# Early-fusion transformer layer on one core: the softmax sums' products beside the value products, three sum buffers, later scaling, and the FFN weights' transposes in the prologue

## The chip, the core and the metric

One core of a Trainium2 chip runs the whole kernel. Its engines run programs of their own and meet at semaphores: PE (TensorE, matrix products into PSUM), ACT (ScalarE), DVE (VectorE), POOL (GpSimd) and SP (SyncE, which here issues every DMA). The metric is the device time of one execution in microseconds (us); less is better.

## What is computed

Sixteen items, each of 1024 image positions (29 features) and 77 text tokens, give 1101 rows of 128 numbers. One attention layer with 8 heads of 64 and one gated FFN with a shared path and 8 experts follow. Cut to what matters:

```python
h = concat([einsum('bsf,fd->bsd', x, W) + pe, text_rows], axis=1)     # 16 x 1101 x 128
y = layernorm(h)
q, k, v = (einsum('bsd,hdk->bhsk', y, w) for w in (wq, wk, wv))
probs = softmax(einsum('bhsk,bhtk->bhst', q, k) / 8)
h = h + concat_heads(einsum('bhst,bhtk->bhsk', probs, v)) @ head_kernel
flat = layernorm(h) * ln_scale + ln_bias
out_shared = swiglu(flat @ shared_in_w.T) @ shared_out_w.T + shared_out_b
routed = cnt @ expert_out_bias                  # the two best experts of the better group
for e in range(8):
    routed = routed + comb[:, e] * (swiglu(flat @ expert_in_w.T) @ expert_out_weight[e].T)
return h + out_shared + routed
```

The text rows come from three tables; one index is a running count modulo 8.

## The kernel before

**Items, steps and tables.** The attention of an item goes by pairs of heads (4), chunks of up to 368 queries (3) and tiles of 128 keys (9): 108 steps. In each step PE makes the scores of one tile for both heads of the pair (`score`, L853 and L855) and ACT their exponentials, `probs` (L960). Behind the scores of its step PE does the work that a table of letters puts there: `k` projections of queries and keys for the next pair (L749), `m` products whose row maxima DVE takes (L758, L1022), `v` values (L742), `p` output projection of the item before (L785), `t`, `g`, `c`, `u` its layer norm, gate and FFN, `x`, `e`, `f` embedding and layer norm of the next item, `r` the row of maxima (L762), `s` the sum's products (L776), and `|` a run of value products (L872). There is a table for the prologue (BEFORE), the first item (FIRST), items 1 to 14 (EVERY), the last (LAST) and the epilogue (BEYOND). `plan` turns a table into a list of units per step, and every engine walks the same list, each in its own order.

**Value products.** A run `|` weighs the values of five tiles (first run of a chunk) or of four (second). Each product writes 64 of the 128 columns of TensorE, so the two heads of a pair run side by side. All other products but the sums' use the whole width.

**Sums.** The softmax denominators of a chunk are added up by POOL, tile by tile, into `sums` (L1246 for the first two tiles, L1250 for the others). At step 3 of the next chunk the unit `s` sums over the partitions with four products of 32 columns each (L776, `ones` as weights). ACT copies the result (L916), SP sends it through a narrow tile (`inv_cols`), DVE inverts it two steps on (`INVERT`), SP stores it and spreads it back over the partitions (`sums<-inverse_rows`). POOL then scales the heads' output (`scale`, L1221). `sums` has two buffers; `scale` of chunk q stands at step 0 of chunk q + 2. The last two chunks of an item are scaled at steps 0 and 8 (`SCALE_LAST`) of the next item, whose projections (`p`) wait for it.

**PSUM.** Two banks hold scores, one the values' output, five (`LANES`) go round among all other units: a unit on PE waits until the unit that had its bank five units before has been read out.

**Startup.** A block of its own loads weights, works out the text rows, transposes the FFN weights on PE (26 transposes, L463) and splits them and the attention weights into a high and a low part (ACT L471 to L484, DVE L556 to L570). All engines meet at its end (L340); then the prologue embeds and norms item 0, projects it and takes the maxima of the first pair.

Of the kernel before, what the change touches and what calls it, by code (L numbers as in the profile page):

```python
# [58 lines left out]
SUM_AT = 3  # L59

PROJ = [4 + j for j in range(NT)]
STATS, TURN, GATE, WEIGHTS = 13, 18, 22, 25
EMBED = 59
MAXROW = 23
STORE = 102
INVERT, SCALE_LAST = 2, 8
# [51 lines left out]
mmmum/mmm/um/msmm/mmm/|mmmumm/mmm/mmu/ummm/  # L118
|mmm/mmmum/mmmu/mmsm/muu/|m/vrvuu/uu/uu/
|uk/ku/uuk/smkm/mkkm/|x/mmem/e/mmm/  # L120
|/mmmum/mmmmu/msm/mmm/mmummm/|mmmmm/mfm/mfuummm/
|mfm/mmm/mmm/msmm/mmmu/m|r/uv/vvuvuv/vvvuv/
k|/kuu/uku/ksmm/kmm/|ku/mmu/mmmm/umm/
|mmm/mmmuu/mmmm/s/mmmmm/m|mmum/umm/mmm/mummm/
m|mm/mmmmu/mmm/msm/mm/r|///
""".split("/")
LAST = """
k/|/k/skmmk/pkmm/pmk|/pmmm/pm/mmpmm/
|pmmm/mpmmmm/p/mpmsm/mmm/|/mmm/mmmm/mmmm/
# [84 lines left out]
def plan(attn, post, prep):  # L214
# [7 lines left out]
    def of_pair(p):  # L222
# [14 lines left out]
        "f": [(("turn1", g), prep) for g in range(3)]}  # L237
# [8 lines left out]
class Segment:  # L246
# [3 lines left out]
    def __init__(self, attn, post, prep, before):  # L250
# [26 lines left out]
def fusion_kernel(nc, x, x_txt, tok_w, pos, nest, seg, txt_w, attn_w, head_w, ln_scale, ln_bias,  # L277
# [40 lines left out]
    counts = sb(ctx, "counts", [P, 12, 32])  # L318

# [7 lines left out]
    raw_loaded = sem("raw_loaded")  # L327
    s_pool = sem("s_pool")
# [11 lines left out]
    with ExitStack() as tmp:  # L340
        attn_raw = sb(tmp, "attn_raw", [P, 3 * H, DH])
        in_raw = sb(tmp, "in_raw", [P, 2, 4, D])
        out_raw = sb(tmp, "out_raw", [P, 1 + E, HID])
# [46 lines left out]
        def _(sp):  # L390
# [16 lines left out]

# [486 lines left out]
    def _(act):  # L894
# [54 lines left out]
        def step(seg, it, b, s):  # L949
# [22 lines left out]
            if seg.post and TURN - 2 <= s <= TURN:  # L972
                normalise(1, b - 1, h_out, s - TURN + 2)
# [433 lines left out]
```

## Time and profile before

| what | us |
|---|---|
| median of 3 runs (4525.02 to 4526.53) | 4525.51 |
| the profiled execution: its own time | 4530.92 |
| its span, first to last instruction | 4529.0 |
| startup block, 0 to 36 | 36.0 |
| prologue, 36 to the first scores at 95.5 | 59.5 |
| first item, 95.5 to about 320 | 224.5 |
| items 1 to 14, about 320 to 4166 | 3846 (274.7 each) |
| last item, to about 4437 | 271 |
| epilogue | 92 |

PE is busy 98% of the span, DVE 71%, POOL 65%, ACT 51%. A busy PE is not a PE at its peak: a product's record lasts about twice as long as the distance to the next product, because products overlap and their ends are modelled. What PE's work costs is therefore read here from the starts: the distance from one start to the next. In a row of the timeline "x8" stands for eight records; a product in plain fp32 leaves two.

The granted clock of PE is 1.00 (2.4 GHz) from 100 us to 4438 but for one short stretch, and moves between the two levels in the startup, the prologue and the epilogue (mean 0.59 from 36 to 95.5).

### The profile page before, as it was taken

How to read it: one execution, taken by the hardware profiler on the slowest of the kernel's cores; microseconds unless marked ns; L12 is line 12 of the kernel's file. 1: busy time of each engine (PE TensorE's matmuls, PEld its weight loads, DVE VectorE, ACT ScalarE, POOL GpSimd, SP SyncE). 2: the span in 40 equal slices, each digit the busy share in tenths (PEclk: the TensorE clock that was granted, in tenths of full speed). 3: DMA queues.
4: the chain of work that ended last, by engine and by line, in shares of the span. 5: the costliest groups of instructions: out<-in, count | busy, mean ns of one | idle time of the engine just before them, and what ended most of it. 6: DMA issues, size and time to landing. Idle time of an engine off the chain costs nothing.

```text
span 4529.0 us, 78729 instructions
## 1 busy us (share of the span) xinstructions
PE 4423.0 (98%) x26589; PEld 3321.9 (73%) x26589; DVE 3226.5 (71%) x7716; ACT 2289.0 (51%) x5638; POOL 2956.3 (65%) x1806
## 2 busy tenths in 40 slices
PE   6999999999999999999999999999999999999997
PEld 4667777777777777777777777777777777777776
DVE  6568777687776877768687776877768677686755
ACT  2554554455544545545555544555545455455542
POOL 1776666666666666666666666666666666666661
PEclk7999999999999999999999999999999999999998
DMA  2111111111101111111111111111111111111000
GB/s 60 36 40 31 33 38 35 38 29 31 47 26 40 33 33 39 33 33 39 38 29 33 40 33 38 29 32 46 27 40 32 34 39 33 33 39 39 23 22 18
DMA packets 156563, 157.33 MB, mean 35 GB/s; under 512 B 66573, under 2 KB 147972, under 8 KB 156164
## 3 DMA queue, kind: packets, MB, share of 16 engines
q1 hardware_dynamic: 156163, 152.29, 13.4%
q8 instruction: 216, 3.54, 0.4%
q14 instruction: 184, 1.50, 0.1%
HBM read 59.25 MB, written 19.65 MB: 17 GB/s over the span
## 4 chain that ended last, share of the span: by engine, by line
PE 87%; DVE 5%; DMA 2%; ACT 2%; issue 1%; SPq 1%; POOL 1%; ACTq 0%; DVEq 0%; POOLq 0%
PE o_ps L872 24%; PE work L758 13%; PE scores L853 13%; PE scores L855 11%; PE work L824 7%; PE work L808 4%; PE work L785 3%; PE work L749 3%; PE work L742 2%; DVE part_max L1022 2%; DMA k_a<-k_a 2%; DVE h_out L1067 1%; PE work L776 1%; PE work L813 1%; ACT probs L960 1%
## 5 line engine op out<-in xcount | busy, mean ns | idle before, releaser
L1250 POOL TENSOR_TENSOR sums<-sums,probs 128x736 f32<-128x736 f32 (+3 forms) x1344 | 2372.5, 1765 | 692.4 <-ACT probs L960 565.2
L960 ACT ACTIVATE probs<-scores 128x368 f32<-128x368 f32 (+3 forms) x3456 | 1459.4, 475 | 1666.6 <-PE scores L855 1598.0
L1022 DVE TENSOR_REDUCE part_max<-work 128x1 f32<-128x368 f32 (+3 forms) x3456 | 1635.4, 530 | 388.1 <-PE work L758 377.3
L853 PE MATMUL scores<-q_a,k_a 128*128 128x368 f32 (+3 forms) x3456 | 1207.3, 349 | 29.2 <-ACT probs L960 21.9
L872 PE MATMUL o_ps<-probs,values 128*64 128x368 f32 (+1 forms) x6912 | 1151.8, 477 | 0.0
L855 PE MATMUL scores<-q_b,k_b 128*128 128x368 f32 (+3 forms) x3456 | 1142.8, 331 | 0.0
L758 PE MATMUL work<-k_a,q_a 128*128 128x368 f32 (+3 forms) x3456 | 925.1, 353 | 16.8 <-DMA k_a<-k_a 11.7
L872 PEld LDWEIGHTS o_ps<-probs,values 128*64 128x64 f32 (+1 forms) x6912 | 462.2, 136 | 534.4 <-issue 476.3
L853 PEld LDWEIGHTS scores<-q_a,k_a 128*128 128x128 f32 (+1 forms) x3456 | 633.6, 183 | 208.1 <-issue 88.6
L758 PEld LDWEIGHTS work<-k_a,q_a 128*128 128x128 f32 (+1 forms) x3456 | 590.0, 185 | 187.7 <-issue 143.3
L855 PEld LDWEIGHTS scores<-q_b,k_b 128*128 128x128 f32 (+1 forms) x3456 | 636.4, 184 | 13.9 <-issue 3.7
L1221 POOL TENSOR_TENSOR heads_t<-sums,heads_t 128x368 f32<-128x368 f32 (+1 forms) x192 | 174.3, 908 | 514.5 <-DMA sums<-inverse_rows 511.7
L1067 DVE SCALAR_TENSOR_TENSOR h_out<-work,comb,h_out 128x128 f32<-128x128 f32 x1152 | 404.2, 351 | 137.3 <-PE work L824 96.8
L1246 POOL TENSOR_TENSOR sums<-probs 128x736 f32<-128x736 f32 (+1 forms) x192 | 340.3, 1772 | 167.4 <-ACT probs L960 148.6
L1012 DVE TENSOR_TENSOR k_b<-work,k_a 64x368 fp32r<-64x368 f32 (+1 forms) x384 | 205.6, 535 | 203.0 <-ACT k_a L911 199.8
L1015 DVE TENSOR_TENSOR q_a<-work,q_a 64x368 fp32r<-64x368 f32 (+1 forms) x384 | 207.1, 539 | 172.5 <-ACT q_a L911 166.5
L824 PE MATMUL work<-down_hi,hid_hi 128*128 128x512 f32 x576 | 231.7, 402 | 0.0
L824 PE MATMUL work<-down_lo,hid_hi 128*128 128x512 f32 x576 | 228.0, 396 | 0.0
L824 PE MATMUL work<-down_hi,hid_lo 128*128 128x512 f32 x576 | 227.6, 395 | 0.0
L911 ACT CAST q_a<-work 64x368 fp32r<-64x368 f32 (+1 forms) x384 | 177.8, 463 | 86.0 <-PE work L749 80.6
L911 ACT CAST k_a<-work 64x368 fp32r<-64x368 f32 (+1 forms) x384 | 176.9, 461 | 85.7 <-PE work L749 80.9
L1055 DVE SCALAR_TENSOR_TENSOR hid<-hid,work 128x384 f32<-128x384 f32 x192 | 106.1, 553 | 79.5 <-PE work L808 71.8
(185 smaller groups left out, 4415.7 us busy)
## 6 DMA issues: line engine op xcount, KB each, us to landing
sums<-inverse_rows SPq DMA_DIRECT2D x190, 184.0 KB
k_a<-k_a SPq DMA_DIRECT2D x128, 184.0 KB, 2.8
q_b<-q_a SPq DMA_DIRECT2D x128, 184.0 KB, 5.3
k_a<-k_a SPq DMA_DIRECT2D x64, 183.0 KB, 2.7
q_b<-q_a SPq DMA_DIRECT2D x64, 183.0 KB, 7.0
resid_rows<-heads_t SPq DMA_DIRECT2D x16, 576.0 KB, 4.5
h_out<-resid_rows SPq DMA_DIRECT2D x16, 576.0 KB, 8.6
heads_t<-in_pe_table_dram SPq DMA_DIRECT2D x16, 512.0 KB
```

What stands on the lines that cost most here:

```text
L758: mm = nc.tensor.matmul(w[0:n, 0:cw], q_a[p % 2][i][:, j * P:j * P + n], k_a[p % 2][i][:, c0:c0 + cw], start=True, stop=True)
L824: mm = nc.tensor.matmul(w, h[:, k2, cols], wt[:, k2, g * EG * D:(g + 1) * EG * D], start=(n == 0), stop=(n == len(ops) - 1))
L853: nc.tensor.matmul(o, k_a[p % 2][i][:, t * P:t * P + n], q_a[p % 2][i][:, c0:c0 + cw], start=True, stop=False)
L855: nc.tensor.matmul(o, k_b[p % 2][i][:, t * P:t * P + n], q_b[:, i, c0:c0 + cw], start=False, stop=True).then_inc(scores_ready, 1)
L872: mm = nc.tensor.matmul(o_ps[64 * i:64 * i + 64, 0:cw], values[0:n, t, h * DH:(h + 1) * DH], probs[0:n, slot(s), i, 0:cw], start=(t == 0), ...
L911: nc.scalar.copy(hi[p % 2][i][0:64, c0:c0 + cw], w[64 * i:64 * i + 64, 0:cw]).then_inc(qk_hi, 1)
L960: nc.scalar.activation(probs[0:n, slot(s), i, 0:cw], scores[0:n, h % SB, 0:cw], ACT.Exp, scale=DH ** -0.5).then_inc(probs_ready, 1)
L1015: ins = nc.vector.tensor_tensor(q_a[p % 2][i][64:128, c0:c0 + cw], src, q_a[p % 2][i][0:64, c0:c0 + cw], ALU.subtract)
L1022: nc.vector.tensor_reduce(part_max[0:n, i * IMG + j if j < IMG else 2 * IMG + i, c:c + 1], w[0:n, 0:keys], AX.X, ALU.max).then_inc(drained ...
L1067: ins = nc.vector.scalar_tensor_tensor(out=o, in0=w[:, e * D:(e + 1) * D], scalar=comb[:, t, g * EG + e:g * EG + e + 1], in1=o, op0=ALU.mu ...
L1246: nc.gpsimd.tensor_tensor(acc, probs[:, slot(s - 1), :, 0:cw], probs[:, slot(s), :, 0:cw], ALU.add).then_inc(sums_done, 1)
L1250: nc.gpsimd.tensor_tensor(acc, acc, probs[0:n, slot(s), :, 0:cw], ALU.add).then_inc(sums_done, 1)
```

## The change

Four parts.

**The sums' products.** In the new tables most `s` units stand directly ahead of a run of five value products, or directly behind it: 131 of the 192 sums (112 in items 1 to 14, eight of twelve in each; nine in the first item, ten in the last). Before, one did, in the epilogue. In items 1 to 14 an `s` so placed stands at step 4, 5 or 6 of its chunk instead of step 3; the one for chunk 4, which stands alone, is at step 8.

**Ring and scaling.** `sums` has three buffers, and POOL scales chunk q at step 4 of chunk q + 2.

**Startup.** The FFN weights land in parts of `hid` and `values`; their transposes are units `w` of the prologue's table, with ACT's and DVE's work on them. The attention weights' low parts are made between the text rows. The count modulo 8 is one bitwise operation instead of nine pairs of comparison and addition. The DMAs stand in another order.

**The five tables** are new in many other places; among them, the prologue's `k` and `v` alternate, and the first `p` of an item moves from step 4 to step 5. Instead of fixed step numbers (PROJ, GATE, EMBED and others) the code looks up where a unit stands; for the units that are not moved this gives the same steps.

```diff
-SUM_AT = 3
+SUM_RING = 3
-INVERT, SCALE_LAST = 2, 8
+INVERT, SCALE_AT, SCALE_LAST = 2, 4, 8
...
 BEFORE = """
...
-/////x/e/e//
-///////f/f/
-f//////v/vvvv/vvvv/
-k/k/k/kmm/kmm/k/mm/mmmm/mm/
+/x/////ee///
+/www//www///w/f/f/
+f///////vkv/vv/
+kv//kvv/mkmm/vkvmm//m/mkmmm/mm/
...
 EVERY = """
-k/|/k/skmmk/pkmm/pmk|/pmmm/pm/mmpmm/
-|pmmm/mpmmmm/p/mpmsm/mmm/|/mmm/mmmm/mmmm/
-tmm|mm/mtmmm/mmtmm/mmsmm/g/r|vv/vv/vv/k/
-u|c/vk/kuu/uskm/kmum|/mmkum/u/mmm/mum|um/
...
-|mmm/mmmum/mmmu/mmsm/muu/|m/vrvuu/uu/uu/
-|uk/ku/uuk/smkm/mkkm/|x/mmem/e/mmm/
+k/|/k/skmm/kmkm/ppmk|/pmmmm/pm/mpmm/
+|pmmm/mpmmmm/p/mpmm/mmm/s|/mmm/mmmm/mmmm/
+tm|mm/mmtmm/mmtmm/mmmmm/g/rs|vv/vv/vv/k/
+u|/cvk/kuu/ukm/kmu|s/mmmkum/u/ummm/mm|u/
...
+|mm/mmmumm/mmmu/mmm/muu/|m/vrvuu/uu/uusk/
+|u/ku/kuum/km/mkk/ms|x/mmem/e/mmm/
...
-            then(nc.vector.tensor_copy(low[:], runs[:]))
-            for m in range(8, TXT + 1, 8):
-                then(nc.vector.tensor_scalar(closes[:], runs[:], float(m), -8.0, ALU.is_ge, ALU.mult))
-                then(nc.vector.tensor_tensor(low[:], low[:], closes[:], ALU.add))
-            nc.vector.tensor_copy(idx[:, 1, :], low[:]).then_inc(s_dve, 1)
+            then(nc.vector.tensor_copy(tok_i[:], runs[:]))
+            then(nc.vector.tensor_scalar(tok_i[:], tok_i[:], 7, None, ALU.bitwise_and))
+            nc.vector.tensor_copy(idx[:, 1, :], tok_i[:]).then_inc(s_dve, 1)
...
-    sums = sb(ctx, "sums", [P, 2, 2, CHUNK])
+    sums = sb(ctx, "sums", [P, SUM_RING, 2, CHUNK])
...
+            elif kind == "weights":
+                if u[1] == 0:
+                    pe.wait_ge(ffn_loaded, 16 * 5)
+                for i, raw in enumerate(weight_groups[u[1]]):
+                    mm = nc.tensor.transpose(w[:, i * P:(i + 1) * P], raw, ident[:])
...
-            if t == 0 and q > 1:
+            if t == SCALE_AT and q > 1:
                 scale(b, q - 2)
...
-                if not isinstance(b, int) or b > 0 or q >= 2:
-                    pool.wait_ge(heads_scaled, PAIRS * NC * b + q - 1)
+                if not isinstance(b, int) or b > 0 or q >= SUM_RING:
+                    pool.wait_ge(heads_scaled, PAIRS * NC * b + q - SUM_RING + 1)
```

On PE, in the second chunk of an item of the loop, the products of the first chunk's sum and the run of five after them. Before:

```order
L776 MATMUL work<-sums,ones 32x184 x4
L758 MATMUL work<-k_a,q_a 128x366
L853 MATMUL scores<-q_a,k_a 128x368
L855 MATMUL scores<-q_b,k_b 128x368
L853 MATMUL scores<-q_a,k_a 128x368
L855 MATMUL scores<-q_b,k_b 128x368
L758 MATMUL work<-k_a,q_a 128x366 x3
L853 MATMUL scores<-q_a,k_a 128x368
L855 MATMUL scores<-q_b,k_b 128x368
L853 MATMUL scores<-q_a,k_a 128x368
L855 MATMUL scores<-q_b,k_b 128x368
L872 MATMUL o_ps<-probs,values 64x368 x10
```

Now, at the same place (the line numbers are those of the changed kernel):

```order
L729 MATMUL work<-k_a,q_a 128x366 x3
L824 MATMUL scores<-q_a,k_a 128x368
L826 MATMUL scores<-q_b,k_b 128x368
L824 MATMUL scores<-q_a,k_a 128x368
L826 MATMUL scores<-q_b,k_b 128x368
L747 MATMUL work<-sums,ones 32x184 x4
L843 MATMUL o_ps<-probs,values 64x368 x10
L824 MATMUL scores<-q_a,k_a 128x368
```

The four products of 32 columns have moved over two steps and stand with nothing between them and the ten of 64.

On POOL, in the third chunk of the first item, the scaling (L1221, then L1218) among the additions of the probabilities. Before:

```order
L1221 TENSOR_TENSOR heads_t<-sums,heads_t 128x368
L1246 TENSOR_TENSOR sums<-probs 128x2x366
L1250 TENSOR_TENSOR sums<-sums,probs 128x2x366 x6
L1250 TENSOR_TENSOR sums<-sums,probs 77x2x366
L1221 TENSOR_TENSOR heads_t<-sums,heads_t 128x368
```

Now:

```order
L1243 TENSOR_TENSOR sums<-probs 128x2x366
L1247 TENSOR_TENSOR sums<-sums,probs 128x2x366 x2
L1218 TENSOR_TENSOR heads_t<-sums,heads_t 128x368
L1247 TENSOR_TENSOR sums<-sums,probs 128x2x366 x4
L1247 TENSOR_TENSOR sums<-sums,probs 77x2x366
```

The scaling has moved behind three additions.

On ACT, from the startup's casts to the first projections of the prologue (`up_hi`, `down_sh` and `down_hi` are the FFN weights, `yt_hi` the normed rows). Before:

```order
L473 CAST wv_hi<-attn_raw 128x512
L478 CAST up_hi<-work 128x512 x2
L484 COPY down_sh<-work 128x128 x2
L484 CAST down_hi<-work 128x128 x16
L340 UNCONDITIONAL_BRANCH
L893 UNCONDITIONAL_BRANCH
L927 COPY normed<-work 128x256
L936 ACTIVATE normed<-heads_t,shift,rstd 128x128 x9
L919 CAST yt_hi<-work 128x384 x3
L905 COPY values<-work 128x256 x9
L911 CAST k_a<-work 64x368 x2
L911 CAST q_a<-work 64x368 x2
```

Now:

```order
L907 COPY normed<-work 128x256
L878 CAST up_hi<-work 128x512 x2
L884 COPY down_sh<-work 128x128 x2
L884 CAST down_hi<-work 128x128 x14
L916 ACTIVATE normed<-heads_t,shift,rstd 128x128 x6
L884 CAST down_hi<-work 128x128 x2
L916 ACTIVATE normed<-heads_t,shift,rstd 128x128 x3
L899 CAST yt_hi<-work 128x384 x3
L876 COPY values<-work 128x256
L891 CAST k_a<-work 64x368 x2
L876 COPY values<-work 128x256 x3
L891 CAST q_a<-work 64x368 x2
```

The FFN casts have moved from ahead of the barrier into the layer norm of item 0, and the first key projection stands behind one copy of values instead of nine.

## Rows read from the trace of the kernel before

**Rows 1.** Busy time by engine, 600 to 4400 us: PE, PEld, DVE, ACT, POOL, clock, DMA.

```profile
600.00:4400.00 3800.00, 3768.68 (x22919) 2841.66 (x22920) 2763.75 (x6570) 1967.77 (x4847) 2553.55 (x1552) 1.00 0.14 35
```

**Rows 2.** Waits of PE, same stretch: us in total, times, longest us.

```profile
PE scores L853 <- ACT probs L960: 13.6, 43, 0.4
PE work L758 <- DMA k_a<-k_a: 8.9, 14, 1.6
PE work L758 <- DVE q_a L1015: 3.4, 14, 0.2
```

**Rows 3.** PE's timeline, a sum's products in the loop: start us, us, what.

```profile
2256.43 0.33 PE L855 MATMUL scores<-q_b,k_b 128*128 128x368 f32 x1
2256.69 0.52 PE L776 MATMUL work<-sums,ones 128*32 128x184 f32 x8
2257.14 0.43 PE L749 MATMUL work<-yt_hi,wqk_hi 128*128 128x368 f32 x1
2257.41 0.33 PE L749 MATMUL work<-yt_lo,wqk_hi 128*128 128x368 f32 x1
2257.58 0.33 PE L749 MATMUL work<-yt_hi,wqk_lo 128*128 128x368 f32 x1
...
2259.83 0.38 PE L785 MATMUL work<-wo,heads_t 128*128 128x128 f32 x2
```

**Rows 4.** PE's timeline, a run of four and one of five value products.

```profile
2251.66 0.33 PE L855 MATMUL scores<-q_b,k_b 128*128 128x368 f32 x1
2251.93 2.68 PE L872 MATMUL o_ps<-probs,values 128*64 128x366 f32 x16
2254.54 0.44 PE L853 MATMUL scores<-q_a,k_a 128*128 128x368 f32 x1
2254.81 0.33 PE L855 MATMUL scores<-q_b,k_b 128*128 128x368 f32 x1
...
2263.89 3.31 PE L872 MATMUL o_ps<-probs,values 128*64 128x368 f32 x20
2267.13 0.44 PE L853 MATMUL scores<-q_a,k_a 128*128 128x368 f32 x1
```

**Rows 5.** Timeline of the startup, DVE and PE.

```profile
9.24 0.19 DVE L518 COPY low<-runs 16x77 f32<-16x77 f32 x1
...
13.85 0.19 DVE L522 COPY idx<-low 16x77 f32<-16x77 f32 x1
...
26.18 0.69 DVE L548 TENSOR_TENSOR text_h<-work,base 77x512 f32<-77x512 f32 x1 [1.02 <-PE work L456]
...
34.67 0.69 DVE L570 TENSOR_TENSOR wv_lo<-attn_raw,wv_hi 128x512 fp32r<-128x512 f32 x1
...
36.04 0.69 PE L831 MATMUL work<-ident,counts 128*128 128x128 f32 x2 [4.39 <-DVE four L1200]
```

**Rows 6.** Waits of SP, first 45 us: us in total, times, longest us.

```profile
SPq L340 <- DMA text_rows<-text_h: 4.3, 1, 4.3
```

**Rows 7.** Timeline from the startup to the prologue, ACT and DVE.

```profile
29.25 3.33 ACT L484 CAST down_hi<-work 128x128 fp32r<-128x128 f32 x16
...
41.07 0.69 DVE L1077 TENSOR_TENSOR heads_t<-work,heads_t 128x512 f32<-128x512 f32 x1 [0.96 <-PE work L835]
...
47.00 3.57 ACT L936 ACTIVATE normed<-heads_t,shift,rstd 128x128 f32<-128x128 f32 x9 [9.80 <-POOL shift L1210]
...
59.95 1.09 DVE L1012 TENSOR_TENSOR k_b<-work,k_a 64x368 fp32r<-64x368 f32 x2 [7.19 <-ACT k_a L911]
...
68.60 22.42 DVE L1022 TENSOR_REDUCE part_max<-work 128x1 f32<-128x368 f32 x50
```

**Rows 8.** POOL's timeline at the start of an item.

```profile
2255.01 0.84 POOL L1221 TENSOR_TENSOR heads_t<-sums,heads_t 128x368 f32<-128x368 f32 x1 [1.81 <-DMA sums<-inverse_rows]
...
2257.91 7.48 POOL L1250 TENSOR_TENSOR sums<-sums,probs 128x736 f32<-128x736 f32 x4
```

**Rows 9.** Groups by line, POOL's scaling: count | busy, mean ns | idle before.

```profile
L1221 POOL TENSOR_TENSOR heads_t<-sums,heads_t 128x368 f32<-128x368 f32 (+1 forms) x192 | 174.3, 908 | 514.5 <-DMA sums<-inverse_rows 511.7
```

More of the change, by code:

```diff
@@ L236, in plan @@
         "e": [(("embed", g), prep) for g in range(2)],
-        "f": [(("turn1", g), prep) for g in range(3)]}
+        "f": [(("turn1", g), prep) for g in range(3)],
+        "w": [(("weights", g), prep and not attn) for g in range(7)]}
     chains["|"] = [(("burst", -1), post)] + [(("burst", n), attn) for n in range(len(GROUPS) * PAIRS * NC - 1)]
@@ L255, in __init__ @@
         self.uses = [0] * LANES
-        self.bank, self.order = {}, {}
+        self.bank, self.order, self.step = {}, {}, {}
         n = 0
-        for units in self.at:
+        for s, units in enumerate(self.at):
             for u in units:
+                self.step[u] = s
+                assert not (middle(u) or u == ("gate",) or u[0] == "sum" and self.prep) or s + 3 < ALL
                 if u[0] == "burst":
@@ L420, in _ @@
             sp.wait_ge(s_stored, 16)
[L421 to L428 removed]
+            sp.wait_ge(raw_loaded, 16 * 16)
         @block.tensor
@@ L458, in _ @@
                 last.then_inc(s_turned, 1)
-            pe.wait_ge(raw_loaded, 16 * 22)
-            for g, group in enumerate(groups):
-                pe.wait_ge(s_taken, 8 + g)
-                for i, (src, _) in enumerate(group):
-                    last = nc.tensor.transpose(work[:, g % LANES, i * P:(i + 1) * P], src, ident[:])
-                last.then_inc(s_turned, 1)
         @block.scalar
         def _(act):
-            act.wait_ge(raw_loaded, 16 * 22)
+            act.wait_ge(attn_loaded, 16)
             v = attn_raw[:].rearrange("p (h w) n -> p w h n", w=3)
@@ L897, in unit @@
             w = work[:, k, :]
-            if kind not in ("v", "qk", "sum", "turn1", "turn2", "count", "up", "turnx") or (kind == "up" and u[4]):
+            if kind not in ("v", "qk", "sum", "weights", "turn1", "turn2", "count", "up", "turnx") or (kind == "up" and u[4]):
                 return
@@ L905, in unit @@
                 nc.scalar.copy(values[:, j, half * HALF:(half + 1) * HALF], w[:, 0:HALF]).then_inc(drained[k], 1)
+            elif kind == "weights" and u[1] < 2:
+                nc.scalar.copy(up_hi[:, u[1]].rearrange("p a n -> p (a n)"), w).then_inc(weights_hi, 1)
+            elif kind == "weights":
+                for i in range(len(weight_groups[u[1]])):
+                    m = 4 * (u[1] - 2) + i
+                    e, k2 = m // KC, m % KC
+                    dst = down_sh[:, k2, :] if e == 0 else down_hi[:, k2, (e - 1) * D:e * D]
+                    ins = nc.scalar.copy(dst, w[:, i * P:(i + 1) * P])
+                ins.then_inc(weights_hi, 1)
             elif kind == "qk":
```

219 lines of the change are left out of this document (104 added, 115 removed).

## The prediction

> **What bounds the kernel now.** I read the busy times of a stretch of the loop first: of 3800 us PE is busy 3768.7, DVE 2763.8, POOL 2553.6, ACT 1967.8 [rows 1]. So PE sets the pace from the first item to the last, and its waits say how strictly: 31.3 us idle in about 13.9 items, 2.3 us an item [rows 1]. The largest are for ACT's exponentials (13.6), the copied half of the keys (8.9) and a split query projection (3.4) [rows 2]. What PE's time is worth can then only be read from the starts of its products. Last I read the startup and the prologue, where PE waits for most of the time: what ends there last is DVE at the barrier and DVE's maxima before the first scores [rows 5, 7].
>
> **A sum's products, alone.** Products of 368 columns start every 0.17 us (2257.41 to 2257.58) [rows 3]. From the score product ahead of the sum (2256.43) to the second product behind it (2257.41) pass 0.98 us; less two starts of 0.17 the sum costs 0.64 [rows 3]. In the same way a run of four value tiles costs 3.15 - 0.34 = 2.81 (2251.66 to 2254.81), and a fifth tile adds 3.24 - 2.61 = 0.63 [rows 4]. Four tiles are 2.52, so the run has 0.29 us that belong to no tile. A sum sends 184 columns where a tile sends 368, in the same two passes, over four quarters of the array instead of two halves: 0.32 of its 0.64. So it has 0.32 that belong to no column. Both pay at the same places: entering costs 0.09 to 0.10 (0.26 and 0.27 to the next start instead of 0.17), leaving the rest, 0.20 to 0.23 [rows 3, 4].
>
> **A sum beside a run.** One leaving and one entering go, and a change from 32 columns to 64 (or back) comes, which no row shows. Its bounds: nothing (0.31 saved: an entering of 0.09 and a leaving of 0.22), or as much as what goes (0 saved). I take 0.10, because entering a narrow form cost the same 0.09 to 0.10 for both widths [rows 3, 4], and what comes is an entering into a narrow form; no wide product follows that would pay for a leaving. Saved: 0.21 each. The 112 in items 1 to 14 give 23.5 us, all on PE's path. Of the 19 others I count 17 (3.6 us); the last two of the last item stand in steps with little other work of PE. Sum 27.1 us, between 0 and 40.
>
> The Trainium skill, TensorEngine Tiling (Array Packing), Tiling Modes, Key Properties, says that changing the tiling mode, not just the tile, drains TensorE, and lists 128x64 and 128x32 as different configurations. By that rule a gap stays between the two neighbours, and the saving is the 27 us of the rows; were the two one mode, it would be 40. The gaps on entering and leaving agree with the rule; the pair of narrow forms no run here shows yet.
>
> **Scaling and ring.** 192 scalings wait 511.7 us for the spread inverses, 2.7 each [rows 9], but POOL has a third of its time free [rows 1], and PE's wait for ACT, which POOL could delay, is 1 us an item [rows 2]. I cost their end at nothing. A later scaling puts 0.9 us [rows 9] behind the third addition of a chunk, where additions follow each other every 1.9 us (7.48 for four) [rows 8]; a third buffer keeps the next chunk's additions free of it. Who waits for POOL? The first projection of an item. Its inverse is there at 2255.0 [rows 8]; the addition of step 3 then ends near 2259.7, the scaling near 2260.7. PE, now at 2259.83 [rows 3], gets there two k, two m and a step's scores later, less the k that stood ahead: about 2261.3. It clears by 0.6 us.
>
> **The other moves in the loop.** The wait for the split query (0.24 us in each of 14 items [rows 2]) goes, since the m behind the last two projections of that chunk now comes after a step's scores: 3.4 us. The stall for the keys' copy stays: the same m stands three steps behind the same k. Against that, PE reaches each row of maxima up to 0.6 us sooner and has five banks to run ahead of DVE. I put 2 us on new waits in all; bounds 0 and 10, the latter 0.7 us an item.
>
> **Startup.** The text chain on DVE loses 18 operations and a copy between 9.24 and 13.85 [rows 5] and gets two of about 0.25: 4.1 us. The last text row, 26.87 now [rows 5], is done at 22.8. The three low parts of the attention weights (0.69 each) fit into the 1.02 us that DVE waits between two text rows [rows 5]. SP stores the rows and waits 4.3 us for them [rows 6]: with its issue, 27.5. Today DVE ends the block at 35.36 [rows 5], because the FFN low parts stand there. Gain 7.9 us. The FFN weights move to the DMAs' end; they are wanted only behind the embedding.
>
> **Prologue.** The FFN casts now lie between embedding and layer norm, where ACT idles 9.80 us [rows 7]. Sixteen small ones took 3.33 [rows 7]; six of the seven groups come to about 5 us, and DVE's add of the embedding (41.07) to ACT's norm (47.00) leaves 5.9 [rows 7]. It fits only just: with five banks the sixth group waits for DVE, which has its statistics first, and the seventh stands between two norms. I put 0.6 us on it (bounds 0 and 5.5). Then DVE's path: it stands idle 7.19 us until the first split key at 59.95, because nine values go ahead on PE and ACT, and works without a pause to 91 [rows 7]. With one value ahead, the key comes up to 4.9 us sooner; but the values between the next projections hold ACT, and I expect DVE to idle about half of that again: 2.5 us gained, between 0 and 4.9.
>
> **Sum.** 27.1 + 3.4 - 2.0 + 7.9 - 0.6 + 2.5 = 38.3 us off the profiled span of 4529.0 (own time 4530.9): 4491. The median of the runs lies 5.4 us under that execution, so I forecast 4525.5 - 38.3, about **4487**.
>
> **Rivals.**
> - *The two narrow forms change for nothing.* 0.31 instead of 0.21 for 129 sums: 13 us more, 4474. For it: their streams look alike in the rows. Against it: both pay on entering, whatever the width.
> - *The change between them costs all that was saved.* 27 us less: 4514. For it: leaving costs twice what entering does, so the price depends on what comes next, and no row has this neighbour.
> - *Slower: DVE and the five banks become the bound.* The sum was also a pause in which DVE caught up with the maxima: 22.42 us for 50, 0.45 each [rows 7], against 0.17 on PE. In the third chunk of an item 15 of them now stand between two runs: 6.8 us for DVE, while PE passes them in four steps of scores (0.68 each) and its transposes in about 5.2. The lag is 1.6; PE stops when it is over five banks, 2.3 us. From there each further microsecond of lag is one of PE's. Were every one of the eight places of an item at that limit, the whole 0.64 of the sum would come back as a wait: 5.2 us an item, 72 in all, 4559. Against it: no such wait of PE stands among the waits [rows 2], and 0.7 us are still free where it is tightest. It takes 2.7 us an item to cancel the gain.
> - *Little is left.* No saving beside the runs, new waits of 5 to 10 us and a slow prologue: 4517 to 4525.
>
> That the change doesn't do what it says can be left out: the order has the sums beside the runs.
>
> **How the numbers follow.** Forecast 0.55 (4478 to 4500 with the bounds of startup and prologue), first rival 0.17, second 0.14, slower 0.07, little left 0.07. The range 4466 to 4516 takes the first three and leaves out the rest. About 0.2%, 9 us, can be told from no change: faster 0.86, same 0.07, slower 0.07.
>
> **What would show it.** In the profile after: from a score ahead of a sum to the second product behind the run about 4.2 us (0.64 + 3.44 - 0.21 and two starts of 0.17; 3.44 is a run of five, 2.81 + 0.63); items of 272.9 us instead of 274.7. The first product of the prologue near 28 instead of 36.04, the first split key near 48 instead of 59.95. POOL's idle time ahead of the scaling near zero. It is wrong if PE's waits name DVE's maxima or POOL's scaling with more than 1 us an item, if a sum beside a run costs as much as apart, or if the norm of item 0 waits for the FFN casts.

## The result: 38 us slower, and where they stand in the profile after

| | before | after |
|---|---|---|
| median, us | 4526.02 | 4564.38 (4562.85 to 4566.91) |
| ratio | 1 | 1.0083, 95% interval 1.0068 to 1.0098 |
| span of the profiled execution | 4529.0 | 4562.8 |
| start to the first scores | 95.5 | 85.3 |
| first item | 230.6 | 229.5 |
| items 1 to 14, each | 274.7 | 278.0 |
| last item and epilogue | 357.6 | 355.4 |

The forecast was 4487. The rows from the first scores on are worked out from the starts of the first score product of each item (14 items: 3845.3 and 3892.6 us). By them the first item before ends at 326.1, not at about 320 as the table ahead of the prediction has it, and the last item starts at 4171, not 4166. Outside the loop the change gained 13.5 us, inside it lost 47.3. The forecast had 24.9 us of gain for the loop, so nearly the whole error of 77 us is there: 5.2 us an item.

The startup went as forecast. DVE's timeline of the changed kernel, startup and prologue (start us, us, what, idle time ahead):

```profile
9.48 0.19 DVE L498 CAST idx<-tok_i 16x77 f32<-16x77 int32 x1
...
21.81 0.69 DVE L526 TENSOR_TENSOR text_h<-work,base 77x512 f32<-77x512 f32 x1 [0.42 <-PE work L452]
...
47.76 1.09 DVE L993 TENSOR_TENSOR k_b<-work,k_a 64x368 fp32r<-64x368 f32 x2 [2.65 <-ACT k_a L891]
```

PE's timeline there:

```profile
28.06 0.69 PE L802 MATMUL work<-ident,counts 128*128 128x128 f32 x2 [6.29 <-DVE four L1197]
...
85.26 0.68 PE L824 MATMUL scores<-q_a,k_a 128*128 128x368 f32 x1 [3.72 <-DMA q_b<-max_rows]
```

The count modulo 8 is done at 9.7 instead of 14 us, the last text row at 22.5 instead of 26.9, PE's first product of the prologue starts at 28.06 instead of 36.04 [rows 5], DVE splits the first key at 47.76 instead of 59.95 [rows 7].

The loop of the changed kernel, 600 to 4400 us, busy times (PE, PEld, DVE, ACT, POOL, clock, DMA):

```profile
600.00:4400.00 3800.00, 3736.59 (x22656) 2809.14 (x22656) 2739.52 (x6531) 1945.05 (x4790) 2505.83 (x1530) 1.00 0.14 34
```

PE's waits in the same stretch (us in total, times, longest us):

```profile
PE work L729 <- DMA k_a<-k_a: 28.2, 27, 1.9
PE work L784 <- DVE part_max L1018: 15.0, 13, 1.2
PE scores L824 <- ACT probs L940: 12.9, 41, 0.4
PE work L729 <- DVE q_a L996: 0.7, 2, 0.4
```

POOL's scaling in the groups by line (count, busy, mean ns, idle before):

```profile
L1218 POOL TENSOR_TENSOR heads_t<-sums,heads_t 128x368 f32<-128x368 f32 (+1 forms) x192 | 173.4, 903 | 95.6 <-DMA sums<-inverse_rows 92.8 <-DVE sums L984 2.7
```

PE is busy 32 us less than in [rows 1], and not because it has less to do: fewer products fit into the stretch (22656 records instead of 22919). Two waits stand out beside [rows 2]: 28.2 us in 27 for the keys' copied half (8.9 in 14 before) and 15.0 us in 13 for a row of maxima, which [rows 2] does not have. Each has one more in every item, 2.5 us an item together of the 5.2. The second comes to 1.1 us an item, over the 1 us that the prediction named as a sign of being wrong. POOL's idle time ahead of the scaling fell from 514.5 to 95.6 us.

What the records of waits hold is not all. Per chunk of an item (mean of items 2 to 14, from the starts of the score products, in us; chunks are counted from 1, steps from 0):

```
chunk      1     2     3     4     5     6     7     8     9    10    11    12    sum
before  23.92 21.36 21.44 26.21 21.26 23.34 24.14 24.17 22.66 23.73 23.26 19.20  274.70
after   23.89 21.14 21.37 27.37 21.38 24.03 23.21 24.26 22.72 26.04 23.53 19.13  278.07
```

A key projection (0.5 us) moved from chunk 7 to chunk 6, and a maximum or two (0.17 each) to a neighbouring chunk; otherwise the chunks have the same work. Chunks 4 and 10 lose 1.2 and 2.3 us. Chunks 5, 8 and 11 each got a sum beside a run, and none is shorter; 5 and 11 hold one maximum more (0.17), 8 does not. Chunk 3, which the prediction's slower rival worked out as the tightest, is 0.07 us shorter and has no wait.

**The sums themselves do what was forecast.** PE's timeline of the changed kernel, second chunk:

```profile
2018.42 0.33 PE L826 MATMUL scores<-q_b,k_b 128*128 128x368 f32 x1
2018.67 0.52 PE L747 MATMUL work<-sums,ones 128*32 128x184 f32 x8
2019.12 3.31 PE L843 MATMUL o_ps<-probs,values 128*64 128x368 f32 x20
2022.37 0.43 PE L824 MATMUL scores<-q_a,k_a 128*128 128x368 f32 x1
2022.64 0.33 PE L826 MATMUL scores<-q_b,k_b 128*128 128x368 f32 x1
```

From the score product ahead (2018.42) to the second behind (2022.64) pass 4.22 us; 4.2 was forecast. Less two starts of 0.17 and a run of five (3.44 from [rows 4]) the sum costs 0.44 us here, 0.20 less than by itself [rows 3].

**The wait in chunk 4.** DVE's timeline of the changed kernel at its end:

```profile
2347.79 0.56 DVE L1051 SCALAR_TENSOR_TENSOR hid<-hid,work 128x384 f32<-128x384 f32 x1
2348.26 1.79 DVE L1083 CAST flat_hi<-normed 128x384 fp32r<-128x384 f32 x1
2350.09 2.05 DVE L1084 TENSOR_TENSOR flat_lo<-normed,flat_hi 128x384 fp32r<-128x384 f32 x1
2352.06 2.32 DVE L1018 TENSOR_REDUCE part_max<-work 128x1 f32<-128x368 f32 x5
```

POOL's timeline there:

```profile
2346.15 5.57 POOL L1247 TENSOR_TENSOR sums<-sums,probs 128x736 f32<-128x736 f32 x3 [0.75 <-ACT probs L940]
```

PE's timeline there:

```profile
2352.64 0.71 PE L784 MATMUL work<-down_sh,hid 128*128 128x128 f32 x4 [1.18 <-DVE part_max L1018]
```

DVE splits the next third of the normed rows into a rounded copy (`flat_hi`) and the remainder (`flat_lo`); below, these two are its copies. They take 1.79 and 2.05 us, and the row of maxima that holds the bank of the shared output's product (L784) comes behind them.

**The wait in chunk 10.** PE's timeline of the changed kernel:

```profile
2475.44 0.33 PE L826 MATMUL scores<-q_b,k_b 128*128 128x368 f32 x1
2477.21 0.41 PE L729 MATMUL work<-k_a,q_a 128*128 128x368 f32 x1 [1.44 <-DMA k_a<-k_a]
```

SP's timeline there, its DMA issues:

```profile
2468.83 0.65 SPq L1285 DMA_DIRECT2D q_b<-q_a  x1
...
2472.09 0.67 SPq L1341 DMA_DIRECT2D k_a<-k_a  x1
```

The new table has two projections at step 0 (`kk`) and the first maximum that needs them at step 2. The copy of the keys' half is issued at 2472.09, behind the copy of the queries and four of maxima; PE waits 1.44 us for it.

### The profile page after: what moved, and what is told of

Its sections match the earlier page's. It is cut to its first block, busy times and chain, and to the rows that moved or that the text cites. A ratio compares the mean times of both kernels' runs of the same rounds, so it can differ in the third digit from the quotient of the medians.

```text
span 4562.8 us, 78693 instructions
## 1 busy us (share of the span) xinstructions
PE 4430.5 (97%) x26589; PEld 3315.0 (73%) x26589; DVE 3217.2 (71%) x7700; ACT 2289.7 (50%) x5638; POOL 2943.0 (65%) x1806
## 4 chain that ended last, share of the span: by engine, by line
PE 85%; DVE 5%; DMA 3%; ACT 2%; issue 1%; SPq 1%; POOL 1%; ACTq 0%; DVEq 0%; POOLq 0%
PE o_ps L843 22%; PE scores L824 13%; PE work L729 13%; PE scores L826 11%; PE work L795 9%; DMA k_a<-k_a 3%; PE work L720 3%; PE work L779 3%; PE work L756 3%; PE work L708 2%; PE work L747 2%; PE work L784 2%; ACT probs L940 1%; DVE part_max L1018 1%; DVE hid L1051 1%
## 5 line engine op out<-in xcount | busy, mean ns | idle before, releaser
L824 PE MATMUL scores<-q_a,k_a 128*128 128x368 f32 (+3 forms) x3456 | 1219.5, 353 | 30.6 <-ACT probs L940 23.0
L729 PE MATMUL work<-k_a,q_a 128*128 128x368 f32 (+3 forms) x3456 | 910.8, 349 | 34.7 <-DMA k_a<-k_a 30.1
L1218 POOL TENSOR_TENSOR heads_t<-sums,heads_t 128x368 f32<-128x368 f32 (+1 forms) x192 | 173.4, 903 | 95.6 <-DMA sums<-inverse_rows 92.8
```

Of the source, the lines that this page charges most:

```text
L729: mm = nc.tensor.matmul(w[0:n, 0:cw], q_a[p % 2][i][:, j * P:j * P + n], k_a[p % 2][i][:, c0:c0 + cw], start=True, stop=True)
L824: nc.tensor.matmul(o, k_a[p % 2][i][:, t * P:t * P + n], q_a[p % 2][i][:, c0:c0 + cw], start=True, stop=False)
```

## The experiments

Theory "placing": the sums are worth 0.20 us each, and the loss stands in single places of the new tables. Against it stood the ring and the later scaling, and the rival of the prediction, in which the sum at step 3 was a pause that DVE (or ACT) needs. Medians are given with the ratio to the kernel before on the same chip.

### The new startup with the old loop, and then the eight sums alone

`e1_old_loop` is the changed kernel with four of its tables put back:

```diff
 EVERY = """
-k/|/k/skmm/kmkm/ppmk|/pmmmm/pm/mpmm/
+k/|/k/skmmk/pkmm/pmk|/pmmm/pm/mmpmm/
...
```

> The changed kernel with the tables FIRST, EVERY, LAST and BEYOND of the kernel before; startup, prologue, ring of three and later scaling stay. Theory 'placing' (what was lost lies in where the loop's tables put units): the 10.2 us that the first scores come earlier stay, items go back to 274.7 us: 4526 - 10 = 4516 us (4511 to 4520). Rival 'ring' (the later scaling or the third buffer slow the loop): items of 276 us or more, 4530 to 4564.

4528.5 us, ratio 1.0003 (0.9994 to 1.0012): between the two theories' ranges. The first scores come at 85.18, as forecast, but items take 275.4. Nearly all of the 0.7 us more is in step 4 of the first chunk (2.50 us before, 3.13 now), and one row of its PE's waits (600 to 4400 us) names it:

```profile
PE work L756 <- POOL heads_t L1218: 7.0, 12, 0.7
```

With the scaling at step 4 the first output projection must not stand in step 4. In the new table it stands in step 5, and there this wait is 0.6 us in the whole stretch. So the later scaling is free only together with that move, and it does not explain the loss.

`e2_beside` then moves eight sums of EVERY ahead of their runs, and maxima (one in chunk 8, three in chunk 11) to steps that this leaves short:

```diff
-|pmmm/mpmmmm/p/mpmsm/mmm/|/mmm/mmmm/mmmm/
+|pmmm/mpmmmm/p/mpmm/mmm/s|/mmm/mmmm/mmmm/
...
-u|c/vk/kuu/uskm/kmum|/mmkum/u/mmm/mum|um/
+u|c/vk/kuu/ukm/kmums|/mmkum/u/mmm/mum|um/
...
-|mmm/mmmuu/mmmm/s/mmmmm/m|mmum/umm/mmm/mummm/
+|mmm/mmmuu/mmm/mmm/mmm/ms|mmum/umm/mmm/mummm/
```

> As e1_old_loop, but in EVERY the eight sums that the change puts beside a run of five value products are moved there, all directly ahead of it, and two steps that this leaves short get a row of maxima from the step ahead. Nothing else moves. Theory 'placing', with 0.20 us saved for each sum: 8 x 0.20 x 14 = 22 us less than e1_old_loop, about 4494 (4489 to 4500), items of 273.1 us. Rival 'no saving' (the change between the two narrow forms costs what the wide one cost): equal to e1_old_loop within 3 us, 4516. Rival 'pause' (the sum's 0.64 us at step 3 was a pause that DVE or ACT needed): 4505 to 4530, with waits of PE for DVE's maxima or ACT's exponentials of more than 1 us an item in steps 1 to 5 of the chunks.

4547.0 us, ratio 1.0042 (1.0030 to 1.0055): 18 us slower than `e1_old_loop`, where the theory wanted 22 less. None of the three forecasts had this. "Pause" came nearest (4505 to 4530), but in the records no wait for maxima or exponentials grew; what grew is the wait for a split query. Step by step (us, mean of items 2 to 14):

```
               step 3         step 4         step 5 (run)    the three together
             e1     e2      e1     e2      e1     e2
chunk 2     2.80   2.15    1.19   1.18    4.12   4.56       -0.22
chunk 4     2.50   1.91    5.57   6.83                      +0.66   (run in step 4)
chunk 5     1.87   1.18    1.17   1.58    5.74   6.07       +0.05
chunk 7     2.16   1.70    2.52   2.97    4.21   4.66       +0.44
chunk 10    2.16   1.51    1.67   2.15    5.20   5.65       +0.28
```

In chunk 2 step 3 gets 0.65 shorter and the run 0.44 longer: the 0.2 of the prediction, in the open. In the other chunks of the table the step behind the sum's old place gets longer by 0.4 to 0.8, beyond a sum that stands in it, and takes it back. Of the three chunks with a moved sum that the table leaves out, chunk 3 gains 0.14, chunk 8 gains 0.02 and chunk 11 loses 0.10. What PE meets in the longer steps is not one thing. In chunk 10, DVE's timeline of `e2_beside`:

```profile
2196.85 0.55 DVE L1051 SCALAR_TENSOR_TENSOR hid<-hid,work 128x384 f32<-128x384 f32 x1
2197.43 1.09 DVE L996 TENSOR_TENSOR q_a<-work,q_a 64x368 fp32r<-64x368 f32 x2
```

PE's timeline there:

```profile
2197.94 0.33 PE L729 MATMUL work<-k_a,q_a 128*128 128x368 f32 x1
2198.58 0.44 PE L729 MATMUL work<-k_a,q_a 128*128 128x368 f32 x1 [0.32 <-DVE q_a L996]
```

The row of this wait in PE's waits of `e1_old_loop`, 600 to 4400 us:

```profile
PE work L729 <- DVE q_a L996: 3.1, 14, 0.2
```

The same row of `e2_beside`:

```profile
PE work L729 <- DVE q_a L996: 13.8, 40, 0.5
```

A maximum waits until the projection one step back has gone through ACT's cast and DVE's split (`q_a`, done at 2198.52). In the item of these rows the wait stands in chunks 4, 7 and 10, with 0.3 to 0.4 us each; in `e1_old_loop` in chunk 7 alone, with 0.2. So the records hold 0.8 us an item of it beyond `e1_old_loop`; the rest of what these chunks lost stands in no record of a wait. In chunk 5 there is no projection, and no wait in the records. DVE's timeline of `e2_beside`:

```profile
2077.00 1.51 DVE L1063 SCALAR_TENSOR_TENSOR h_out<-work,comb,h_out 128x128 f32<-128x128 f32 x4 [0.21 <-PE work L795]
2078.42 3.20 DVE L1018 TENSOR_REDUCE part_max<-work 128x1 f32<-128x368 f32 x7
```

PE's timeline there:

```profile
2078.39 0.33 PE L826 MATMUL scores<-q_b,k_b 128*128 128x368 f32 x1
...
2078.93 0.96 PE L729 MATMUL work<-k_a,q_a 128*128 128x366 f32 x3
```

DVE first adds an expert's four products (1.51 us) and starts the maxima of step 3 (2078.42) when PE is already at the scores of step 4; from then on seven follow each other every 0.45 us. PE's three take 0.80 to the next start (2078.93 to 2079.73) instead of three times 0.17.

### Less work for DVE

`e6_half_old` and `e7_half_beside` are the same two kernels with maxima over half of the columns:

```diff
-                keys = min(CHUNKS[c][1], T - CHUNKS[c][0])
+                keys = min(CHUNKS[c][1], T - CHUNKS[c][0]) // 2
```

> e1_old_loop with maxima over half of their columns only (the rest of the row is left out), so that DVE has less to do in the loop and PE as much as before. Its wait for POOL's scaling (0.64 us an item) stays. It is the other half of the comparison with e7_half_beside; by itself 4500 to 4528: at the upper end if DVE holds PE nowhere in these tables.

> e2_beside with maxima over half of their columns, as in e6_half_old. Theory 'DVE' (what ate the saving of the eight sums is that the sum at step 3 gave DVE time to catch up): with DVE light the saving appears, 8 x 0.20 x 14 = 22 us less than e6_half_old (18 to 24). Rival 'ACT' (it is ACT's exponentials and casts, which are as long as before): equal to e6_half_old or up to 18 us above it, as with whole maxima.

4509.2 (0.9961, 0.9948 to 0.9973) and 4518.6 us (0.9981, 0.9972 to 0.9990). One maximum takes 340 ns instead of 529. The line of the maxima in `e1_old_loop` (min/median/max ns, first and last start):

```profile
L1018 DVE TENSOR_REDUCE part_max<-work x3456: 484/529/544, 52.9 to 4370.6; 128x1 f32<-128x368 f32 x192
```

The same for `e6_half_old`:

```profile
L1018 DVE TENSOR_REDUCE part_max<-work x3456: 294/340/352, 52.7 to 4349.0; 128x1 f32<-128x184 f32 x192
```

10 us of each time are the prologue's, where the first scores now come at 75.0 and 74.9. The difference between the two tables shrinks from +18 to +9 us: theory "DVE", which wanted 22 less, fails, and the rival "ACT" (0 to 18 more) has it in its range. But the shorter maxima did take half of the loss away. Chunk 5 now shows its saving (21.29 to 21.13), chunk 8 too (24.25 to 24.10): there it was DVE's maxima. Chunks 4, 7 and 10 still lose 0.46, 0.46 and 0.32 (0.62, 0.45 and 0.30 with whole maxima). There PE's waits still name the split query, whose way through ACT and DVE did not get shorter; `e6_half_old` has no such wait. The row of `e7_half_beside`:

```profile
PE work L729 <- DVE q_a L996: 12.1, 39, 0.5
```

That is 0.9 us an item.

### The two waits of the new table

```diff
-kk|/u/mkuu/kum/kmmm/s|u/muk/mmmm/um/
+kk|/u/kuu/mkum/kmmm/s|u/muk/mmmm/um/
```

> The changed kernel with one row of maxima of the tenth chunk in EVERY moved from step 2 to step 3. Theory 'placing': its wait for the keys' copied half (1.55 us, 1.7 with what the records hide) goes and no other comes, and the tenth chunk falls from 26.04 us to 24.2 to 24.5: 14 x 1.7 = 24 us less than the changed kernel's 4564, 4540 (4534 to 4546). Rival 'shifted' (PE only meets the next wait a step on, ACT's or DVE's): 4552 to 4564.

4544.5 us, ratio 1.0038 (1.0025 to 1.0050): 20 us less. The tenth chunk falls from 26.04 to 24.55. PE's wait for the copy goes back to 9.0 us:

```profile
PE work L784 <- DVE part_max L1018: 14.9, 13, 1.2
...
PE work L729 <- DMA k_a<-k_a: 9.0, 15, 1.6
```

```diff
-u|/cvk/kuu/ukm/kmu|s/mmmkum/u/ummm/mm|u/
+u|/cvk/kuu/ukm/kmu|s/mmmkum/u/mmm/mum|u/
```

> The changed kernel with the last FFN unit of the fourth chunk in EVERY moved from step 7 to step 8, where the kernel before has it. Theory 'placing': DVE's two copies of the normed rows (1.80 and 2.05 us now) again start behind the maxima of that step, the first of them in about 0.4 us beside an idle POOL, and PE's wait of 1.16 us ahead of the shared output goes: 14 x 1.2 = 17 us less than 4564, 4547 (4542 to 4553). Rival 'shifted' (the copies then hold the maxima of the next chunk and PE waits there): 4556 to 4564.

4545.2 us, ratio 1.0041 (1.0028 to 1.0053): 19 us less. DVE's timeline of `e4_u_later` at that place:

```profile
2062.08 1.83 DVE L1018 TENSOR_REDUCE part_max<-work 128x1 f32<-128x368 f32 x4
2063.83 0.54 DVE L1051 SCALAR_TENSOR_TENSOR hid<-hid,work 128x384 f32<-128x384 f32 x1
2064.29 0.35 DVE L1083 CAST flat_hi<-normed 128x384 fp32r<-128x384 f32 x1
2064.68 1.98 DVE L1084 TENSOR_TENSOR flat_lo<-normed,flat_hi 128x384 fp32r<-128x384 f32 x1
```

Four maxima now stand ahead of the copies, and the first copy takes 0.35 us instead of 1.79. POOL is not idle there, though the expectation had it so. In each of 13 items this copy starts 0.03 to 0.06 us ahead of POOL's next addition; in the changed kernel it starts 0.16 to 0.53 us behind the start of one. The wait of L784 is gone from the records.

With both, `e5_both`:

> The changed kernel with both moves, that of e3_m_later and that of e4_u_later. If the two waits are independent, their savings add up (19.9 and 19.2 us): 4564 - 39 = 4525 us (4521 to 4530), items of 275.1 us. That would be the items of the kernel before and not 1.6 us less, so the sums' saving would still have to be lost elsewhere. Rival 'one cause' (both come from the same lag of DVE): 4535 to 4545.

4527.8 us, ratio 1.0000 (0.9991 to 1.0009). The two add up: 37 us of the 39. Items take 275.4. That is still 2.3 us above the 273.1 that the sums should have given.

### What remains in the loop

`e11_half_both` takes the shorter maxima to `e5_both` (the edit is that of `e6_half_old`).

> e5_both with maxima over half of their columns (the rest of the row is left out). With its two waits repaired e5_both still has items of 275.4 us where 8 x 0.20 less than 274.7 would be 273.1. Of the shorter maxima 10 us show in the prologue, as in e6_half_old. Theory 'DVE' (the rest is DVE's maxima): items of 273.1, 4528 - 10 - 32 = 4486 (4482 to 4492). Rival 'chain' (the rest is projections on their way through ACT and DVE, and steps shorter than ACT's exponentials allow): items of 274.4 to 274.9 as e7_half_beside lost about 1 us, 4500 to 4510.

4502.1 us, ratio 0.9948 (0.9935 to 0.9960): in the rival's range, and 16 us above theory "DVE". Items take 274.3, 1.1 us less; `e6_half_old` gained 0.7 an item with the old tables, so 0.4 at most is DVE's maxima in places that only the new tables have.

`e10_behind` asks whether the losses of chunks 4, 7 and 10 go when the maxima are moved behind the run. Its base is `e8_mixed`, the changed kernel with chunks 4 to 12 of EVERY put back:

```diff
-u|/cvk/kuu/ukm/kmu|s/mmmkum/u/ummm/mm|u/
...
-m|mm/mmmmu/mmm/msmm/m/r|///
+u|c/vk/kuu/uskm/kmum|/mmkum/u/mmm/mum|um/
...
+m|mm/mmmmu/mmm/msm/mm/r|///
```

> The changed kernel, but in EVERY only its first three chunks (two sums beside runs, the first output projection at step 5); the other nine are those of the kernel before. From the steps measured in the single runs: 23.89 + 21.14 + 21.37 for the three chunks instead of 66.72, so items of 274.4 us, and the earlier start and the new first and last items: 4526 - 10 - 5 + 2 = 4513 us (4509 to 4517). If the chunks hang together more than their single times say: 4520 or more.

4515.2 us, ratio 0.9976 (0.9966 to 0.9986), in its range; but the items take 274.7 and not 274.4. What it gains on the kernel before stands outside the loop: in the profiled executions 10.6 us up to the first scores, 1.3 in the first item and 4.0 behind the loop.

```diff
-u|c/vk/kuu/uskm/kmum|/mmkum/u/mmm/mum|um/
+u|c/vk/kuu/ukm/kmus|/mmmkum/u/mmm/mum|um/
...
-|uk/ku/uuk/smkm/mkkm/|x/mmem/e/mmm/
+|uk/ku/uuk/mkm/mkk/s|xm/mmem/e/mmm/
...
-k|/kuu/uku/ksmm/kmm/|ku/mmu/mmmm/umm/
+k|/kuu/uku/kmm/k/s|mmku/mmu/mmmm/umm/
```

> e8_mixed with three more sums beside their runs of five (chunks 4, 7 and 10 of an item), and in the same chunks the maxima that stood between a fresh projection and that run are moved behind the run. Theory 'chain' (what e2_beside lost in these chunks, 0.3 to 0.6 us each, is PE arriving at a row of maxima before its projection has gone through ACT's cast and DVE's split, for which the sum had given time): no such wait is left, 0.20 us saved in each, and in chunk 7 also the old wait of 0.24: 14 x 0.84 = 12 us less than e8_mixed's 4515, about 4504 (4500 to 4509). Rival 'DVE' (DVE is full there and holds PE wherever the maxima stand): 4515 to 4530.

4517.1 us, ratio 0.9980 (0.9971 to 0.9989): no gain in all, which is in the range of the rival "DVE", and each chunk has its own answer. Chunk 7 gained 0.20 (24.15 to 23.95), the sum's saving; "chain" wanted 0.24 more from its old wait, and that did not come though the wait is gone from the records. Chunk 10 did not move (23.69 to 23.72), and why stays open. Chunk 4 lost 0.19, and there the sum itself waits, for the bank of a projection that DVE has not split yet. PE's waits of `e10_behind`:

```profile
PE work L747 <- DVE q_a L996: 4.3, 13, 0.3
```

`e12_ninth` puts chunk 10 of `e5_both` into that order:

```diff
-kk|/u/kuu/mkum/kmmm/s|u/muk/mmmm/um/
+k|/kuu/uku/kmm/k/s|mmku/mmu/mmmm/um/
```

> e5_both with the tenth chunk of EVERY in the order of the kernel before, the sum ahead of its run and the two maxima of step 4 behind the run. That chunk took 24.51 us in e5_both and 23.72 with one row of maxima more in e10_behind. If the loss stands in that chunk's own order, it falls to 23.55: 14 x 0.96 = 13 us less than e5_both's 4528, 4515 (4511 to 4519). If what it loses comes back in the next chunk, 4522 to 4528.

4513.1 us, ratio 0.9970 (0.9960 to 0.9981). Chunk 10 falls from 24.51 to 23.53 and no other chunk moves by more than 0.04. So this is the new table with all its eight sums beside runs, repaired in two chunks: 13 us faster than before.

### Steps that are shorter than ACT allows

`e9_moved` changes two things in `e8_mixed` that have nothing to do with the sums:

```diff
-k/|/k/skmm/kmkm/ppmk|/pmmmm/pm/mpmm/
+k/|/k/sk/kmmkmm/ppmk|/pmmmm/pm/mpmm/
...
-|mfm/mmm/mmm/msmm/mmmu/m|r/uv/vvuvuv/vvvuv/
+|mfm/mmm/mmm/msmm/mmmu/m|r/uv/vvuvuv/vu/
...
-m|mm/mmmmu/mmm/msm/mm/r|///
+m|mm/mmmmu/mmm/msm/mm/r|/v/v/v/
```

> e8_mixed with two moves that have nothing to do with the sums. The first two maxima of an item go from step 3 to behind a projection of step 4, where the keys' copied half has landed (0.64 us of wait now); three value units of the next item go from chunk 9 to the last three steps of chunk 12, which hold scores alone and take 1.25 us where their products take 0.69. If those steps are as long as ACT's exponentials allow, a value's 0.35 us fits in: 0.6 + 3 x 0.3 = 1.5 us an item, 21 us, 4494 (4488 to 4500). If ACT's copy of the values (0.37 us) lengthens them: 0.6 us an item, 4507.

4508.5 us, ratio 0.9966 (0.9952 to 0.9980). The first move was wrong: step 4 of the first chunk then waits about 1.2 us for a split query, and the chunk loses 0.50. PE's waits of `e9_moved`, 600 to 4400 us:

```profile
PE work L729 <- DVE q_a L996: 18.7, 28, 1.3
```

The second is free: chunk 9 falls from 22.62 to 21.56, and chunk 12 stays at 19.22 (19.24) with three values more. So the time is near the 4507 of the expectation by other terms: a full gain of the second move and a loss by the first.

`e13_best` leaves the first move out and takes chunk 7 from `e10_behind`; `e14_six` moves six values:

```diff
-|mfm/mmm/mmm/msmm/mmmu/m|r/uv/vvuvuv/vu/
+|mfm/mmm/mmm/msmm/mmmu/m|r/uv/vuvu/u/
...
-m|mm/mmmmu/mmm/msm/mm/r|/v/v/v/
+m|mm/mmmmu/mmm/msm/mm/r|/vv/vv/vv/
```

> e8_mixed with what paid in the single runs: the three values in the last steps of chunk 12 (chunks 9 and 12 of e9_moved, 1.08 us less) and the sum of chunk 7 beside its run with the last maxima behind it (0.20 less in e10_behind). 14 x 1.28 = 18 us less than 4515: 4497 (4492 to 4502). If the gains hang together (ACT), 4502 to 4510.

> e13_best with six values in the last three steps of chunk 12 instead of three. Two values make a step's products 1.39 us, 0.14 more than its 1.25, and take 0.35 each from chunk 9: 3 x 0.21 x 14 = 9 us less than e13_best, 4488 (4483 to 4494). If ACT, which copies the values between its exponentials, lengthens these steps to 1.6 us or more: e13_best's time or above.

4499.6 (0.9942, 0.9929 to 0.9956) and 4488.3 us (0.9915, 0.9901 to 0.9928). ACT's timeline in the last steps of an item, `e8_mixed`:

```profile
2236.21 0.84 ACT L940 ACTIVATE probs<-scores 128x366 f32<-128x366 f32 x2 [0.41 <-PE scores L826]
2237.41 0.84 ACT L940 ACTIVATE probs<-scores 77x366 f32<-77x366 f32 x2 [0.36 <-PE scores L826]
```

The same steps in `e14_six`:

```profile
2220.74 0.84 ACT L940 ACTIVATE probs<-scores 128x366 f32<-128x366 f32 x2 [3.84 <-PE scores L826]
2221.47 0.65 ACT L876 COPY values<-work 128x256 f32<-128x256 f32 x2
2222.13 0.84 ACT L940 ACTIVATE probs<-scores 128x366 f32<-128x366 f32 x2
2222.85 0.66 ACT L876 COPY values<-work 128x256 f32<-128x256 f32 x2
```

Busy times of `e14_six`, 600 to 4400 us:

```profile
600.00:4400.00 3800.00, 3784.98 (x23041) 2855.26 (x23040) 2753.84 (x6579) 1967.96 (x4857) 2562.89 (x1562) 1.00 0.14 35
```

With scores alone a step lasts 1.20 to 1.25 us (2236.21 to 2237.41), though its products take 0.69: ACT needs 0.84 for the two exponentials and then waits 0.36 to 0.41 for the next scores, which wait for a bank of scores. ACT's copy of two values (0.65) goes into this gap, and the three steps take 1.48, 1.37 and 1.37. So chunk 12 grows by 0.4 us (19.24 to 19.66) and chunk 9 falls by 2.05 (22.62 to 20.57). In the loop PE is busy 3785.0 us of 3800, against 3768.7 before [rows 1]. `e14_six` beats both kernels: 38 us less than before.

## Why the prediction was wrong, point by point

**What bounds the kernel.** PE does, and its 3768.7 of 3800 us were read rightly. But DVE's 2763.8 (73%) and the "2.3 us an item" of PE's idle time are means, and the change works inside single chunks. The kernel before, busy times of chunks 5 and 4 of one item (same columns as above):

```profile
2068.18:2089.44 21.26, 21.26 (x122) 16.86 (x122) 16.71 (x42) 8.28 (x20) 14.21 (x9) 1.00 0.05 13
2041.95:2068.18 26.23, 26.23 (x159) 19.35 (x160) 24.17 (x49) 16.41 (x40) 18.12 (x11) 1.00 0.30 72
```

In chunk 4 DVE is busy 24.2 of 26.2 us, and it is there that a delay of DVE reached PE. The prediction did not read DVE's busy time by chunk.

**A sum alone and beside a run.** Right: 0.64 and 0.44, a saving of 0.20 for a forecast of 0.21. The change between the two narrow forms is not free, which agrees with the rule of the Trainium skill (TensorEngine Tiling (Array Packing), Tiling Modes, Key Properties) that a change of mode drains TensorE: both neighbours here are different modes, and from the start of the sum's products (2018.67) to that of the run (2019.12) pass 0.45 us, as much as to a wide product in [rows 3] (2256.69 to 2257.14). What falls away is the run's own entering (0.09) and the late second start behind the sum (0.10). Both rivals on this point are out: a change for nothing would leave 0.33, one that costs all that was saved 0.64.

**That the saving is PE's path.** This step failed: "The 112 in items 1 to 14 give 23.5 us, all on PE's path". The sum at step 3 was also the time in which maxima were taken and projections went through ACT and DVE. `e2_beside` shows it: the run grows by 0.44 for a sum of 0.64, and still 1.1 us an item were lost instead of 1.6 gained. In the changed tables, repaired in two chunks (`e12_ninth`), items take 274.4 instead of 273.1: 1.3 us an item of the saving did not come.

**New waits.** This step failed by more. The prediction puts 2 us on them, at most 10. The loop came out 5.2 us an item above the forecast, 72 in all. Three places make 3.9 of it, 54 us: the copied keys in chunk 10 (1.5 an item by `e3_m_later`), the copies of the normed rows in chunk 4 (1.4 by `e4_u_later`), and the order of projections and maxima in chunk 10 (1.0 by `e12_ninth`). The prediction says of the keys' copy that "the same m stands three steps behind the same k". That holds for chunk 1, where the wait of before stands; in chunk 10 it is two steps now. Of DVE's copies it says nothing. Of the remaining 1.3 us an item shorter maxima explain 0.4 at most (`e11_half_both`). The cause of the rest stays open; projections on their way and steps that became shorter than ACT allows are candidates that no run separates.

**Scaling and ring.** Costed at nothing, and right with the first output projection at step 5; with it at step 4 it costs 0.6 us an item (`e1_old_loop`). POOL's idle time ahead of the scaling is 95.6 us, not quite near zero.

**The other moves.** The wait for the split query went from 3.4 to 0.7 us, as forecast.

**Startup and prologue.** 10.2 us gained for a forecast of 9.8, and its marks came within 0.3 us: 28.06 for 28, 47.76 for 48. The norm of item 0 did not wait for the FFN casts: from DVE's add of the embedding to it pass 5.93 us, as before. The granted clock from PE's first product to the first scores was 0.69, and 0.59 before; how much of the prologue's 2.2 us is the clock's was not separated.

**The rivals.** The slower one named 4559 and a chance of 0.07. Its time is near by luck: its mechanism, DVE's maxima and the five banks at all eight places, is only a part. With maxima a third shorter the eight sums still cost 9 us. It had no room for a projection on its way, for a copy by DMA, or for DVE's copies beside POOL. The chance for the slower side was too small for a change of five tables, since each moved unit is a place of its own.

## What to carry to other kernels

A saving on the busiest engine is only worth what the next one behind it allows in that stretch: read the busy times chunk by chunk, and for each moved unit look up what it waits for and who waits for its bank. In a kernel whose order is a table, change one row of it at a time, since the gains of single moves added up here within some microseconds, and so did the losses. A step that is held by another engine's pace is a place for free work.

## What the runs showed of the hardware

The time of DVE's two copies of normed rows, from SBUF to SBUF, depends on whether POOL is in an instruction when they start. Of the 39 `flat_lo` in items of the changed kernel between 600 and 4100 us, 26 started while POOL was adding: each ended 0.4 us after that addition ended, and they took 2.0 us on average; the other 13 took 0.56. For `flat_hi` the 13 free ones took 0.35 us; 13 ended 0.2 us after POOL's addition, with 1.4 to 1.8 us, and 13 ended 0.2 us after POOL's scaling, which had started a moment before them, with 1.15 us. The maxima, which read PSUM, took 483 to 544 ns throughout. The Trainium skill (SBUF — State Buffer, Who interferes with whom) says that DVE and POOL share a pair of ports by an exclusive lock, that copies and casts in a two-port mode contend for it, that operations with two inputs in SBUF contend with POOL's reads, and that reductions never contend; these rows agree. Here the place of such a copy on DVE, not its size, sets its price: 0.35 or 1.79 us for the same instruction, and between the two (`e4_u_later` and the changed kernel) its start moved by only about 0.2 us against POOL's.
